# Weights of the last 50 expert tiles: copied on chip by VectorE from all eight experts, in place of one load for each tile

## The reference

```
logits = h @ W_router + b_router          # 8 experts, 8192 rows h of 128
top2, weights p1, p2 = softmax of the two largest
y[e]   = relu(h @ W1[e] + b1[e]) @ W2[e] + b2[e]      # 128 -> 512 -> 128
out    = x + gate * (p1 * y[first] + p2 * y[second])
```

## Time and profile before

| | |
|---|---|
| median of 3 runs | 1633.04 us (1629.73 to 1641.36) |
| span of the profiled execution | 1622.0 us; its own time is not given beside it, so it is set against the median, 11.0 us above the span |
| busy over the span | PE 83%, DVE 68%, ACT 61%, POOL 34% |
| weight loads (in_wexp) | 109 + 31 + 16 = 156, 514.0 KB each |
| DMA | 217.68 MB, 134 GB/s over the span |

### The profile page before, as it was taken

The page is one execution under the profiler, slowest core; times in us unless marked ns, Lnnn a source line. Parts: engine busy times, 40 slices in busy tenths (PEclk is TensorE's granted clock), DMA queues, the critical chain, the costliest instruction groups (busy, mean ns, idle before and its releaser), DMA issues.

```text
span 1622.0 us, 26719 instructions
## 1 busy us (share of the span) xinstructions
PE 1353.9 (83%) x8354; PEld 866.5 (53%) x8354; DVE 1095.2 (68%) x2943; ACT 990.8 (61%) x2295; POOL 545.8 (34%) x589
## 2 busy tenths in 40 slices
PE   3466897889888888999999979899899998998681
PEld 1234454534445444666666644467566754687571
DVE  5568879788989898676876895967755754140113
ACT  1354765667676556877777766567568565555430
POOL 2123222313122475212112256435322134344335
PEclk7677998989999889999999998799999999999885
DMA  4012135142321424454544524256555556788772
GB/s 126 7 36 72 42 114 167 46 132 64 110 77 30 121 83 116 139 157 124 168 134 141 154 87 137 78 164 193 159 169 171 159 166 207 225 275 276 225 244 76
DMA packets 202037, 217.68 MB, mean 134 GB/s; under 512 B 17419, under 2 KB 167526, under 8 KB 199593
## 3 DMA queue, kind: packets, MB, share of 16 engines
q1 hardware_dynamic: 193704, 199.18, 41.0%
q0 software_dynamic: 8192, 16.79, 3.4%
HBM read 161.18 MB, written 53.94 MB: 133 GB/s over the span
## 4 chain that ended last, share of the span: by engine, by line
PE 43%; DVE 21%; issue 11%; ACT 8%; POOL 7%; DMA 6%; SPq 2%; POOLq 0%; ACTq 0%; another core or an unknown queue 0%; DVEq 0%
DVE cmx L1581 6%; PE bank L1228 5%; PE bank L1045 5%; PE bank L1028 5%; PE bank L1212 5%; PE bank L1196 4%; PE bank L1151 3%; PE bank L1124 2%; POOL kg L775 2%; DMA kg<-y_slots,sslot 2%; PE bank L1164 2%; PE bank L1013 2%; POOL bhs L775 2%; ACT wide L903 2%; PE bank L1140 2%
## 5 line engine op out<-in xcount | busy, mean ns | idle before, releaser
L1581 DVE TENSOR_REDUCE cmx<-bank 128x2 f32<-128x512 f32 x512 | 328.7, 684 | 97.4 <-PE bank L1196 89.3
L903 ACT ACTIVATE wide<-bank 128x512 f32<-128x512 f32 x512 | 280.0, 609 | 69.2 <-PE bank L1212 64.6
L1212 PE MATMUL bank<-wide 75*128 75x512 bf16 x512 | 174.9, 407 | 23.2 <-DVE cmx L1581 14.7
L1196 PE MATMUL bank<-wide 72*128 72x256 bf16 x1024 | 176.2, 283 | 20.6 <-DVE cmx L1581 15.6
L756 POOL DMA_INDIRECT x_slots<-sx,sslot x128 | 128.1, 1001 | 111.3 <-issue 46.9
L1196 PEld LDWEIGHTS bank<-wide 72*128 72x128 bf16 x1024 | 92.0, 101 | 124.7 <-issue 48.2
L1228 PE MATMUL bank<-wide,bva 128*32 128x512 f32 x1024 | 146.5, 646 | 9.9 <-ACT wide L903 5.7
L942 ACT ACTIVATE mH<-bank,mW 128x128 f32<-128x128 f32 x376 | 107.0, 371 | 57.8 <-PE bank L1028 50.9
L1028 PE MATMUL bank<-mT,mW 128*128 128x128 f32 x872 | 123.8, 287 | 17.0 <-DMA mW<-in_wexp 7.9
L1028 PEld LDWEIGHTS bank<-mT,mW 128*128 128x128 f32 x872 | 112.6, 199 | 36.3 <-issue 14.7
L775 POOL DMA_INDIRECT kg<-y_slots,sslot x88 | 85.9, 976 | 117.9 <-DMA kg<-y_slots,sslot 35.6
(11 more groups left out here) (296 smaller groups left out, 2863.4 us busy)
## 6 DMA issues: line engine op xcount, KB each, us to landing
mW<-in_wexp SPq DMA_DIRECT2D x109, 514.0 KB
...
inner<-in_wexp SPq DMA_DIRECT2D x31, 514.0 KB
wide<-in_wexp SPq DMA_DIRECT2D x16, 514.0 KB
...
```

The source lines that it names most:

```text
L903: act.activation(cP[:, i % 8, :], bank[seat["G_s", i]][:, :], ACT.Exp, scale=SCALE).then_inc(S["c_p"], 1)
L1196: ins = pe.matmul(ps[:, j * T:(j + 1) * T], cQ[0:SROWS, z, h, tt * P:(tt + 1) * P], cK[0:SROWS, z, h // G, :], start=True, stop=True)
L1212: pe.matmul(ps[:, :], cK[0:KROWS, z, g, sc_ * P:(sc_ + 1) * P], cQ[0:KROWS, z, h0:h0 + 2, :], start=True, stop=True).then_inc(S["c_s2"], 1)
L1581: dve.tensor_reduce(cmx[:, u % 2, tt, 2 * hp:2 * hp + 2], bank[seat["C_s", i]][:, :].rearrange("p (j t) -> p j t", j=2), AX_X, ALU.max, ne ...
```

## The change

The eight slots in `wide` go. In their place, once the attention has finished with `wide`, eight plain loads (`M_e`) bring the weights of all eight experts there, `experts`. Tiles up to 105 still load their weights with `M_w`. From tile 106 (COPIED_TILE) on, 50 tiles, VectorE reads the offset of the tile's expert from a new table `seo` and copies 1028 columns from `experts` into one of the six slots in `inner` and `mW` (`M_c`). `S_tile` has one more instruction for `seo`. SyncE's list has 106 `M_w` and 8 `M_e` where it had 156 `M_w`, VectorE's has 50 `M_c` more, and the lists of all engines are written anew, with many small shifts.

```
-INNER, WIDE = 4, 8
+INNER = 4
+COPIED_TILE = LATE_TILE + 12
...
-SLOTS = 2 + INNER + WIDE
+SLOTS = 2 + INNER
...
-        weights += [wide[:, k * WROW:(k + 1) * WROW] for k in range(WIDE)]
...
+        experts = wide[:, 0:EXPERTS * WROW]
...
             if t < LATE_TILE:
                 w_slots.append(t % 2)
-            elif t < FIRST_TILE[-1]:
+            else:
                 w_slots.append((2 + t - LATE_TILE) % (2 + INNER))
-            else:
-                w_slots.append((2 + INNER + t - FIRST_TILE[-1]) % SLOTS)
...
+                    if s == "M_e":
+                        if i == 0:
+                            sp.wait_ge(S["c_pv"], CHUNKS * BC * 4)
+                        sp.dma_start(experts[:, i * WROW:(i + 1) * WROW],
+                                     a["wexp"][i * P:(i + 1) * P, :]).then_inc(S["m_e"], 16)
...
+                        dve.tensor_scalar(seo[:, i, 0:w_], sef[:, 0:w_], WROW / P, None, ALU.mult).then_inc(S["s_tile"], 1)
...
+                    if s == "M_c":
+                        t = COPIED_TILE + i
+                        g = place(t)[0]
+                        j = t - FIRST_TILE[g]
+                        k = w_slot(t)[0]
+                        if i == 0:
+                            dve.wait_ge(S["m_e"], 16 * EXPERTS)
+                        dve.wait_ge(S["s_tile"], 3 * (g + 1))
+                        dve.wait_ge(S["m_y"], w_before(t) + 1)
+                        at = dve.value_load(seo[0:1, g, j:j + 1], min_val=0, max_val=(EXPERTS - 1) * WROW)
+                        dve.tensor_copy(weights[k], experts[:, bass.ds(at, WROW)]).then_inc(S[f"m_w{k}"], 16)
```

More of the change, by code:

```diff
@@ L330, in program @@
         sef = sb("sef", [P, SLOT_TILES])
-        sei = sb("sei", [P, GROUPS, SLOT_TILES], I32)
+        sei, seo = (sb(n, [P, GROUPS, SLOT_TILES], I32) for n in ("sei", "seo"))
         sx = sb("sx", [P, 2, NT, D])
@@ new lines @@
+        B_ldm A_ldm A_ldg A_ld A_ldm B_st B_ldm G_ldm A_ldg A_ld B_stq C_ld*2 A_ldm B_st B_ldm Z C_row A_ldg
+        A_ld B_stq C_ld C_row A_ldm B_st C_ld B_stq C_row A_ldg B_ldm G_st A_ld G_ldm Z K_ldx R_ldm R_st S_ld
+        C_ld A_ldm B_ldm C_row B_st C_ld Z B_stq G_ldm C_row G_st A_ldg A_ld R_ldm R_st S_ld C_ld C_row B_ldm
+        B_st A_ldm C_ld Z G_ldm C_row R_ldm R_st A_ldg A_ld B_stq C_ld G_st C_row B_ldm B_st A_ldm C_ld G_st
+        G_ldm C_row R_st R_ldm A_ldg A_ld B_stq C_ld C_row B_ldm B_st C_ld A_ldm G_st G_ldm C_row R_st R_ldm
@@ new lines @@
+        B_ldm C_row M_st M_w B_st M_ldx M_w*2 K_st K_ldx M_w C_ld M_w M_st M_ldx M_w*2 G_st C_row M_w G_ldm M_w
+        M_st R_st R_ldm M_ldx B_stq M_w*2 C_row C_ld M_w*2 M_st M_ldx M_w*3 B_st C_ld M_w M_st M_ldx M_w G_ldm
+        C_row M_w G_st M_w R_st R_ldm M_w M_st M_ldx B_stq C_row M_w C_ld M_w*3 M_st S_ld M_w C_row M_w C_ld M_w
+        S_ld G_st G_ldm M_w M_st M_w*6 R_st R_ldm C_row M_st S_ld M_w M_ldx*6 M_w*4 M_st K_st M_e*6 M_ldx M_e
+        M_w M_e M_w K_ldx M_st G_st M_ldx M_st M_ldx R_st S_ld K_st K_ldx M_st M_ldx M_st K_ldx K_st M_st*2
@@ new lines @@
+        S_sc B_ln A_ln B_ln A_h E_ln2 A_ln E_dx2 B_sub*2 E_dx R_ln R_hn E_out B_ln A_ln B_ln A_h E_ln2 A_ln
+        E_dx2 B_sub*2 E_dx R_ln E_out R_hn B_ln A_ln B_ln A_h E_ln2 A_ln E_dx2 E_dx R_ln R_hn E_out B_ln A_ln
+        B_sub*2 A_h E_ln2 A_ln E_dx2 R_ln E_dx R_hn B_ln E_out S_sc*2 B_sub A_ln S_sc B_sub B_ln S_sc*2 A_h
+        E_ln2 S_sc A_ln E_dx2 S_sc B_ln E_dx S_sc*3 R_ln E_out R_hn A_ln B_sub*2 B_ln K_g*2 B_ln A_h E_ln2 A_ln
+        K_g E_dx2 B_sub K_g B_sub E_dx K_g R_ln K_g R_hn E_out B_ln K_g*2 E_ln2 K_g E_dx2 B_ln K_g E_out R_ln
@@ L1779 @@
+        R_hn B_sub B_ln B_sub B_ln R_ln R_hn B_sub*2 S_sc*6 R_ln S_sc R_hn S_sc K_g*3 R_ln K_g R_hn K_g*2 S_sc*4
+        K_g*16
         """,
@@ new lines @@
+        E_exp R_h G_s*5 B_n0 G_s G_o G_s*2 B_h G_s*2 A_n0 R_e G_s G_o B_w1*3 C_mt B_w1 G_s*7 B_n1 G_s*5 G_o
+        G_s*2 B_h2 G_s*2 E_n2 A_n1 G_o E_xn2 G_ct A_xn E_fk*4 R_n E_fr C_mt B_split R_h E_r B_split G_s*7
+        B_split G_s*4 R_e G_o G_s*4 B_n0 G_s E_exp G_o B_h A_n0 B_w1*4 C_mt G_s*9 G_o G_s*6 B_n1 G_s E_n2 B_h2
+        G_o E_xn2 A_n1 G_ct A_xn E_fk*4 R_n E_fr C_mt R_h E_r G_s*5 R_e G_s B_split G_s*4 B_split G_o G_s*4 B_n0
+        B_split G_s*2 E_exp B_h G_o A_n0 B_w1*4 C_mt G_s*11 G_o B_n1 G_s*5 E_n2 G_o B_h2 A_n1 E_xn2 G_ct A_xn
@@ new lines @@
+        A_xn M_u G_ct E_fk M_d E_fk*2 M_u E_fr R_n M_d C_mt M_t E_r M_u G_s*5 M_d G_s*3 M_u B_n0 G_s M_d G_s G_o
+        G_s R_h G_s*2 B_h E_exp M_u G_s*3 R_e M_d A_n0 B_w1 M_u G_o M_d B_w1 M_t B_w1 M_u B_w1 M_d M_u M_d C_mt
+        M_u B_n1 M_d B_h2 M_u G_s E_n2 G_s*2 M_d G_s*2 A_n1 G_s*2 E_xn2 M_t G_s*2 B_split M_u G_s G_o G_s
+        B_split G_s M_d G_s*3 M_u A_xn B_split E_fk M_d G_s E_fk M_u G_o E_fk M_d E_fk M_u E_fr G_ct C_mt M_d
+        M_t M_u R_n G_s*2 M_d G_s*2 M_u E_r G_s*2 M_d G_s*2 R_h B_n0 G_s*3 G_o G_s M_u A_n0 R_e G_s M_d G_s*3
@@ new lines @@
+        B_w20 B_w21 E_xn2 A_xn E_fk*2 B_h2 E_fk B_q E_fk E_fr B_q E_vk0 B_k E_vk1 E_r B_v E_k E_v B_h B_w1*3
+        E_wo B_w1 C_s*3 B_w20 C_s B_w21 E_xn2 C_s*5 E_fk A_xn C_s*2 E_fk C_s E_fk*2 C_s E_fr C_s*3 E_vk0 B_h2
+        E_vk1 B_q C_mt C_s*2 E_r C_s E_k C_s*2 E_v B_q G_s*3 B_k G_s*4 G_pv G_s*3 B_v G_s G_pv G_s*4 C_s G_o G_s
+        C_s*2 G_pv C_s G_pv C_s*4 B_h C_s*3 B_w1 G_o C_mt B_w1*2 G_s*3 B_w1 G_s*3 B_w20 C_s*3 E_wo G_s B_w21
+        C_s*2 G_pv C_s G_s*2 E_xn2 G_pv G_o G_s C_s G_s B_h2 E_fk C_s*3 B_q E_fk G_s E_fk B_q G_pv B_k G_s*3
@@ new lines @@
+        C_s*3 B_x2 G_o C_s*2 B_ln1s E_rec E_att E_x1 E_ln2s B_q G_o C_s A_ln1s B_q C_s B_k C_s*3 G_o C_s*2 B_v
+        C_s*2 E_mix2 C_s*2 G_y C_mp R_ln C_s*4 E_mix C_s*2 R_c E_out C_s B_ln0s R_lg R_m1 E_scan R_m2 R_e G_o
+        C_s R_info C_s E_y C_s*7 E_wkv C_mp E_wkv1 E_wkv2 G_o C_s A_ln0s C_s E_rec E_att C_s A_c B_x2 B_ln1s
+        E_x1 E_ln2s A_ln1s B_q*2 G_o C_s B_k E_mix2 C_s*4 B_v C_s*4 G_o C_s*2 G_y C_s R_ln C_s E_mix C_mp C_s
+        R_c C_s E_out C_s*3 E_scan B_ln0s E_y A_ln0s R_lg R_m1 G_o R_m2 R_e E_wkv E_wkv1 E_wkv2 C_s*2 E_rec
@@ L1950 @@
+        K_out M_c*8 K_sum M_c*2 K_out M_c*3 K_sum M_c K_out M_c*4 K_sum M_c K_out M_c K_sum K_out K_sum K_out
+        K_sum K_out K_sum K_out
         """,
```

368 lines of the change are left out of this document (165 added, 203 removed).

## The result

The changed kernel takes 1676.55 us (median of 4 runs, 1671.31 to 1684.44) where the kernel before took 1631.38 beside it: ratio 1.0262, with a 95% interval of 1.0221 to 1.0303. It is slower by 2.6%, 45 us. The profiled execution took 1684.44 us with a span of 1682.6.

The account below looks back on a forecast made before the run. GpSimd's chain of gather batches was taken to bound the end; its last group starts 11.4 us earlier, lock cost of 6 us included, so 1633.0 - 11.4 = 1621.6, say 1622 us; range 1604 to 1643 us.

Parts of the forecast that it names:

- the sum: Whole kernel: the last group's first gather starts at 1582.5 us against 1593.87, 11.4 us earlier; the 28.1 us behind stay.
- the 6 us: First 1400 us: lists written anew may move the attention's end by 6 us either way; counted in the range only.
- rival 3: Start of copied part: eight loads land at 1430 to 1435 us, TensorE waits 8 to 13; 1630 to 1635 us; chance 0.16.
- The copy: VectorE from tile 106: 1028 columns take 0.69 us as one-source float32 work; upper bound 1.23 us from the two-source operation.
- The pitch: VectorE from tile 106: one copy every 1.15 us with register read and address, at most 2.5 us.
- K_g14: 15th batch of gathers, where GpSimd's continuous chain begins: starts at 1440.5 us, 9.5 us later than before.
- Six batches to K_g16: GpSimd's chain after its start: 7.0 us a batch without weight loads, ending at 1482.5 us (1484.91 before).
- K_g18 to K_g28: GpSimd's later gather batches, up to the last group's first gather: 70 us, from 1506.5 to 1576.5 us.
- the lock: Copies against gathers in the last stage: gathers wait for VectorE copies, 6 us in all, between nothing and 35.
- Rival 2: Last stage: gathers and copies fall into step, costing up to 35 us in place of 6; 1651 us; chance 0.10.
- TensorE's last quad: End of TensorE's tiles: last quad stored by 1571 us, landed 5 us before the last group's first gather at 1576.5.
- rival 1: Last stage: copies and gathers don't meet, TensorE becomes the bound; gain of 23 us, 1610 us; chance 0.32.

Follow-up runs that it names:

- e1: Changed kernel with the earlier kernel's step lists up to the attention's end, copies and their new list end behind; 0.9914 of the kernel before.
- the other heads: Old lists and copies as in e1, with steps in front of the gather batch K_g14 reordered in three ways; 0.9937, 0.9920 and 0.9919 of the kernel before.
- e2: Kernel before, weights loaded for all 156 tiles, with the changed kernel's step lists up to the attention's end; 1.0287 of the kernel before.
- e4: Changed kernel with 20 scatter steps of the first two groups back at their old places in GpSimd's list; 1.0384 of the kernel before.
- e3: Changed kernel with only SyncE's list of the kernel before in front, all other lists new; 1.0407 of the kernel before.
- e7: Changed kernel with only TensorE's old list up to the attention's end; 1.0518 of the kernel before.
- e8: Copies behind; up to the attention's end every engine's list halfway between old and new places; 1.0461 of the kernel before.
- e15: Copies behind; up to the attention's end all lists three tenths of the way from old to new; 1.0242 of the kernel before.
- e6: Changed kernel with old lists of GpSimd, ScalarE and VectorE up to the attention's end, TensorE and SyncE new; 1.0322 of the kernel before.
- e5: Copies behind; new lists of all engines until chunk 8's A and E steps, old ones from there to the attention's end; 1.0081 of the kernel before.
- e12: Old lists with copies as in e1, plus 14 pauses of eight register reads in TensorE's program, no step moved; 1.0386 of the kernel before.

## Why the prediction was wrong

**The step that failed** is the last sentence of the sum: "The lists were also written anew for the 1400 us before; small swaps like these may move the attention's end by 6 us either way". They moved it by 68.8 us in the profiled execution, of which some 15 us lie in which executions were profiled; new lists with loads cost 47 us in the medians (0.0287 x 1632). I had looked at the diff of the lists, found shifts by a place or two (0.22 places on TensorE in the mean, 2.2 on SyncE), and took them for nothing with a margin. No row stood behind the 6 us. Neither the forecast nor a rival held this case (the range had 6 to 8 us for it), that the order in front and not the copies decides. The profile did hint at it. TensorE is busy for 90% of those 1153 us, and its waits in front of one line are 34 of at most 1.5 us, so it had little slack in which a shift could vanish; and the earlier trace rows show the clock of a stretch in which it pauses (0.82).

**What stood**, by the sum's own steps:

- M_e landed later than said by little: first copy 20.2 us behind the attention's end, 18.5 predicted for the landing. That no cover is there was right too, and so was rival 3's remark that tile 104's weights stand behind seven M_e: they took 11 us to land, but TensorE waited only 1.55 us of them.
- The copy: 0.697 us, predicted 0.69 from the earlier trace rows; the two-source upper bound of the earlier trace rows was never near. The pitch I put too high: 0.79 us for copies in a row, not 1.15, since the read hides, the lower of the two ends that I gave for the earlier trace rows.
- K_g14: 38.1 us behind the attention's end, predicted 37.0. The cost of the new order at this place was found by listing every step that it was moved past.
- Six batches to K_g16: 46.3 us where 42 stood (54 before), so 7.7 a batch and not 7.0. K_g16 to K_g18 21.4 for 24. K_g18 to K_g28 76.3, predicted 70 and most of 6 for the lock.
- The lock: 8.4 us, predicted 6 between 0 and 35 from the earlier trace rows. More were touched than the chance of 0.24 for a start inside a copy says: 30 of the 72 ran beside one for a part of their time, at 0.29 us each. Rival 2's falling into step didn't happen.
- TensorE's last quad 18 us ahead of K_g28, predicted 11.5; rival 1's bound by TensorE stayed away. K_g28 to the end 28.2.

From the attention's end on the prediction has 207.1 us and the trace 210.3. Before it was 218.5, so the gain there is 8.2 us and not 11.4. With old lists in front and the forecast's own end behind, e1 gains 14 us in the medians (9 to 19 by its interval), and the other heads gain 10 to 16 us, which the forecast's 11.4 meets.

**What stays open.** That the lists lose is shown by e1 and e2, and how by the windows: TensorE pauses for 30 us more, and the clock falls with it. Why just this old set fits, and which of the 335 moved steps of SyncE or the 469 of VectorE start it, isn't settled. The one place that I named and mended (e4) gave nothing back and got a wait of the same kind; the mixtures e3, e7, e8 and e15 were worse than their nearest end, and e6 was no better. All of them lie between these two sets, and no third set was tried. e5 shows only that both halves of the way take part. The clock's own part is shown by e12 for pauses that I made; that the longer busy time of the new lists has the same cause is argued from the same two numbers in the same window, and its size (36.8 us in one pair, 1.5 in another) isn't settled.

**How a rule and the rows compare on the clock.** From 250 us to the attention's end the kernel before has some 115 us at 1.2 GHz and the one after 220, and the busy time rises by 36.8 us. The Trainium skill, TensorE: Matmul & The Clock Gate, "Terms", puts the penalty of throttled time at about the time multiplied by one minus the ratio; by it my estimate for 105 us more is 52 us. The rows show less. With a clock given to 0.01 the estimate is good to 12 us, and that TensorE isn't busy for all of the time at the low clock could be the rest; no run here shows it.
